# Six window-attention and gated-MLP layers behind a linear-attention layer: norm spreading and mask by 32-row tiles, one score product instead of two for a chunk's first 32 queries, no one-column products, K normalised behind the output projection

## Chip, core and metric

One core of one Trainium2 chip runs the whole program. The metric is the device time of one execution in microseconds (us). A core has five engines with queues of their own: PE (TensorE, matrix products), DVE (VectorE), ACT (ScalarE), POOL (GpSimd) and SP (SyncE, which issues all the DMAs here). They meet only through semaphores.

## What is computed

A token sequence of 2048 x 128 passes a linear-attention layer once and then six layers (DEPTH = 6) of local attention and a gated MLP. The changed part is in the local attention, 16 heads of 64, windows of 32 tokens that look one window back:

```python
q = l2norm(q) * qs
k = l2norm(k) * ksc
q = q * cos * scale + rotate_half(q) * sin * scale
inv = 1.0 / scale
k = k * cos * inv + rotate_half(k) * sin * inv
...
mask = (it < jb) | (it > jb + w) | (jb == -1)
sim = jnp.einsum('bhwie,bhwje->bhwij', bq, bk2) * QK_SCALE
sim = jnp.where(mask, -jnp.finfo(sim.dtype).max, sim)
attn = jax.nn.softmax(sim, -1)
out = jnp.einsum('bhwij,bhwje->bhwie', attn, bv2)
...
x = attn_layer(shift_tokens(x), Wqkv[i], q_scale[i], k_scale[i], Wo[i]) + x
x = ffn_layer(x, ...) + x
```

## The kernel before

The start (matrix names `m_...`) normalises the input and computes the linear attention of all 2048 tokens. Then a software pipeline runs over N = 48 blocks of T = 256 tokens (eight in each layer). One step of the pipeline is one block's projections (parts `a_...`), the attention of the block before it (`b_...`) and the MLP of the one before that (`c_...`). The order within a step is one table, SCHEDULE (line 57); every engine's code walks the same table and takes the parts that it has. EARLY (line 65) lists the parts of block 0 that are written out by hand in the start instead. All queues are in order.

The parts that matter here, for a block m:

- `a_v`, `a_x`, `a_y` (lines 414 to 459): V projection, and the two rotary halves of four head groups p = 0 to 3 (0 and 1 are K, 2 and 3 are Q), each into PSUM bank 0 (x) and bank 1 (y). Each operand is split in a high and a low part, so a product is three passes (`xh,wh`, `xh,wl`, `xl,wh`).
- `a_mx`, `a_my` (DVE, line 774) multiply the banks by the rotary tables into UV, `a_sqx`, `a_sqy` (ACT) square them, `a_rot` (POOL, line 1170) adds the halves into Kt or Qt.
- `a_norm` (line 461) sums the squares by head, `a_rck`, `a_lnk` make the inverse root R, `a_rh`, `a_rl` split it. `a_sp` (line 475) spreads R over the partitions with a selection matrix `sel`: part b fills bank b with four products of 128 rows. `a_kn` (DVE, line 818) multiplies Kt by bank b. Since banks 0 and 1 are taken by this, `a_x(m, 3)` waits for `a_kn(m, 0)` (semaphore khat_done) and `a_y(m, 3)` for `a_kn(m, 1)`.
- SP then copies the normalised K (`keys`, line 308: 8 DMAs, waits for both `a_kn`) and Q (`queries`, line 320: 8 DMAs) into the layout Kb, Qb, and V into the window layout V2 (`windows`, line 283: 16 DMAs, waits for `a_vs`).
- `b_s` (line 495): mask and scores of a chunk of 128 queries. The mask is added first, by products with an identity (`identb`), in 32x32 tiles, 8 for a chunk. The scores are 64 products a chunk and half (`i`) of 32 queries by 64 keys in 64x32 tiles. A chunk's first 32 queries of a block need the last 32 keys of the block before, kept apart in Kh, so they take two products of 32 keys each.
- `b_pt`, `b_pto` transpose the attention weights, `b_att` multiplies by V (64x64 tiles), `b_oto` (ACT) copies the result out, and `b_wo`, `c_wo` are the output projection. `b_att` begins chunks with a one-column product (line 550) that carries a wait.

On PE the order around the change is: `b_att`, `c_h0`, `a_sp0`, `a_sp1`, `b_wo`, `a_x3`, `a_y3`, `b_pt2`.

Of the kernel before, what the change touches and what calls it, by code (L numbers as in the profile page):

```python
# [17 lines left out]
P = 128  # L18
S = 2048
# [37 lines left out]
SCHEDULE = """a_vs0 a_v0 a_vs1 b_lnq a_sqy0 a_sqx0 b_rcq a_v1 a_mx0 a_rot0 a_x0 a_my0 b_sub0 b_rq w_h1 b_scale0 a_sqy1  # L57
    b_max0 c_xs b_exp0 a_mx1 a_rot1 a_y0 c_xb b_nrm0 c_zsq a_sqx1 a_halo a_xs+1 a_my1 c_rs b_sum0 b_s0 b_scale1
    a_lnk b_rqt b_s1 a_sqy2 a_x1 b_pto0 b_sub1 c_zh a_rh a_y1 c_wo c_zl b_s2 c_mu b_s3 c_var a_norm0 a_x2 b_pto1
    a_rl a_rck a_y2 b_pt0 b_exp1 a_rot2 a_sqx2 b_max1 b_oto0 c_zn a_mx2 a_my2 b_sum1 c_gelu0 b_pt1 b_att0 b_nrm1  # L60
    b_att1 c_h0 w_l0 a_sp0 a_rot3 a_kn0 w_h0 a_xh+1 a_sp1 b_wo a_kn1 a_xl+1 a_x3 a_sqy3 b_pto2 a_y3 b_pt2 c_hm0
    c_h1 a_mx3 a_my3 w_l1 b_att2 c_hm1 c_gelu1 b_xb a_sqx3 b_pt3 c_h2 b_pto3 c_hm2 a_norm1 c_gelu2 b_att3 c_wh
    c_wl w_h2 c_fin c_down w_l2 b_oto1""".split()
LAG = {"w": 0, "a": 0, "b": 1, "c": 2}
EARLY = """a_xs0 a_xh0 a_xl0 a_halo0 a_v0 a_vs0 a_v1 a_vs1 a_x0 a_y0 a_mx0 a_my0 a_sqy0 a_sqx0 a_rot0
    a_x1 a_y1 a_mx1 a_my1 a_sqy1 a_sqx1 a_rot1 a_norm0 a_sum0 a_rck0 a_lnk0 a_rh0 a_rl0 a_sp0 a_sp1 a_kn0 a_kn1""".split()
# [64 lines left out]
def program(nc, a):  # L131

    with ExitStack() as ctx:
# [19 lines left out]
        Kt = sb("Kt", [P, 2, HQ, T])  # L153
        Kb = sb("Kb", [P, HP, T])
        Kh = sb("Kh", [P, HP, W])
# [26 lines left out]
        identb = sb("identb", [P, P], BF16)  # L182
        ident = sb("ident", [P, P])
# [37 lines left out]
        Kst = Kt[:, :, :, :].rearrange("p h q t -> p (h q) t")  # L221
# [15 lines left out]
        def _(e):  # L237
# [98 lines left out]
            tables(1)  # L336
            keys(0)
            e.wait_ge(s["x1_done"], G1)
            e.dma_start(a["scratch"].rearrange("(c p) n -> p c n", p=P), xt).then_inc(s["scratch_out"], 16)
            e.wait_ge(s["scratch_out"], 16)  # L340
            for m in range(N):
# [7 lines left out]
                windows(m)  # L349
                if m:  # L350
                    keys(m)
# [16 lines left out]
        def _(e):  # L368
# [106 lines left out]
            def a_sp(m, b):  # L475

                e.wait_ge(s["rl_done"], m + 1)
                if b == 0:
                    e.wait_ge(s["sq_done"], m * 8 + (6 if m else 4))
                else:  # L480
                    e.wait_ge(s["mul_done"], m * 16 + (12 if m else 8))
                for i in range(2):
                    out = ps[:, b, i * T:(i + 1) * T]
                    mm(out, sel[:, 2 * b + i, :], Rh[:, :], True, False)
                    ins = mm(out, sel[:, 2 * b + i, :], Rl[:, :], False, True)
                ins.then_inc(s["rkb_done"], 1)
# [8 lines left out]
            def b_s(n, i):  # L495
# [5 lines left out]
                if i % 2 == 0:  # L501
# [28 lines left out]
            def b_pt(n, i):  # L530
# [597 lines left out]
        def _(e):  # L1128
# [126 lines left out]
```

## Time and profile before

| | |
|---|---|
| median of 3 runs | 1840.32 us (1836.89 to 1849.28) |
| the profiled execution's own time | 1832.69 us |
| span of the profile (first to last instruction) | 1831.1 us |
| busy: PE, DVE, ACT, POOL | 1654.4, 1217.9, 1139.4, 1000.9 us |
| mean granted TensorE clock | 0.969 of 2.4 GHz |

The profile is that of one execution. Busy time of PE is the union of its products' times; a product's end is modelled and overlaps the next ones, so for PE the distance from start to start is what to read. A product in fp32 stands as two instructions in the trace, so counts there are twice those of the code. "Idle before" is the engine's idle time ahead of an instruction, with what ended it. SPq rows are DMA issues of SP.

### The profile page before, as it was taken

What the parts mean: (1) busy time and instruction counts of PE and PEld (TensorE: products, weight loads), DVE (VectorE), ACT (ScalarE), POOL (GpSimd) and SP (SyncE); (2) the same over time, 40 slices, a digit from 0 to 9 for tenths busy, and PEclk for the clock granted to TensorE, in tenths of its full rate; (3) what the DMA queues carried; (4) which work ended last, traced back from release to release, by engine and by line L of the source; (5) the groups of instructions that cost most, each with busy time, mean ns of one, the idle gap of its engine ahead of it and who ended that gap; (6) DMA issues with size and microseconds to landing.
All of it is one profiled execution on the core that took longest, in us unless ns stands there. A gap on an engine that the chain in (4) does not pass through costs nothing.

```text
span 1831.1 us, 80253 instructions
## 1 busy us (share of the span) xinstructions
PE 1654.4 (90%) x35762; PEld 1360.0 (74%) x35762; DVE 1217.9 (67%) x1910; ACT 1139.4 (62%) x2115; POOL 1000.9 (55%) x757
## 2 busy tenths in 40 slices
PE   5858999989989998899999999999999989999986
PEld 4447778777777877778777787777778777778775
DVE  7656677666657766666766775676677676677562
ACT  2225676657656766666766666576566676667653
POOL 2135466656545656655674664585566475566441
PEclk9979999999999999999999999999999999999996
DMA  3085665665655567556557655557655665665650
GB/s 124 12 199 126 165 145 132 149 170 127 152 136 134 127 157 194 114 130 158 133 125 194 154 129 138 139 130 188 162 129 128 152 141 123 154 152 127 140 120 24
DMA packets 98585, 253.25 MB, mean 138 GB/s; under 512 B 30016, under 2 KB 36288, under 8 KB 97472
## 3 DMA queue, kind: packets, MB, share of 16 engines
q1 hardware_dynamic: 98240, 248.12, 56.8%
q8 instruction: 281, 4.60, 1.1%
q14 instruction: 64, 0.52, 0.1%
HBM read 44.59 MB, written 2.10 MB: 25 GB/s over the span
## 4 chain that ended last, share of the span: by engine, by line
PE 54%; DVE 11%; issue 9%; ACT 9%; SPq 8%; DMA 2%; POOL 0%; ACTq 0%; DVEq 0%; POOLq 0%
PE ps L370 49%; DVE E L841 4%; SPq L317 4%; PE ps L539 4%; SPq L328 4%; DVE rs L851 3%; DVE UV L780 2%; ACT E L930 2%; ACT zs L930 2%; DMA Qtb<-Qtb 2%; ACT PT L930 1%; ACT sq L930 1%; ACT Vs L930 1%; PE ps L492 1%; ACT R L930 1%
## 5 line engine op out<-in xcount | busy, mean ns | idle before, releaser
L780 DVE SCALAR_TENSOR_TENSOR UV<-ps,veca,rope 128x512 f32<-128x512 f32 x768 | 526.7, 743 | 192.4 <-PE ps L370 191.5
L1183 POOL TENSOR_TENSOR Kt<-UV 128x512 f32<-128x512 f32 x192 | 240.8, 1275 | 446.5 <-DVE UV L780 445.3
L930 ACT ACTIVATE sq<-ps 128x512 f32<-128x512 f32 (+1 forms) x400 | 231.5, 579 | 321.7 <-PE ps L370 303.4
L1183 POOL TENSOR_TENSOR Qtb<-UV 128x512 f32<-128x512 f32 x192 | 242.6, 1286 | 123.5 <-DVE UV L780 123.5
L1193 POOL TENSOR_TENSOR E<-E,mx 128x1024 f32<-128x1024 f32 x96 | 182.7, 1903 | 148.4 <-DVE mx L847 148.4
L370 PE MATMUL ps<-xh,wh 128*128 128x256 f32 x768 | 242.2, 315 | 6.0 <-issue 4.4
L370 PE MATMUL ps<-xh,wl 128*128 128x256 f32 x768 | 221.9, 289 | 1.8 <-issue 1.8
L370 PE MATMUL ps<-xl,wh 128*128 128x256 f32 x768 | 221.5, 288 | 1.9 <-issue 1.9
L370 PEld LDWEIGHTS ps<-PT,V 64*64 64x64 f32 x12288 | 198.7, 135 | 31.6 <-issue 19.3
L370 PE MATMUL ps<-Kb,Qtb 64*32 64x64 f32 (+1 forms) x12288 | 189.3, 223 | 34.6 <-issue 34.5
L370 PE MATMUL ps<-PT,V 64*64 64x32 f32 x12288 | 215.9, 221 | 1.5 <-ACT PT L930 0.7
L370 PEld LDWEIGHTS ps<-Kb,Qtb 64*32 64x32 f32 x12288 | 154.0, 106 | 63.2 <-issue 63.0
L370 PE MATMUL ps<-OT,wo 128*128 128x128 f32 x1536 | 194.8, 281 | 4.4 <-issue 4.4
L1202 POOL TENSOR_TENSOR E<-E,ri 128x1024 f32<-128x1024 f32 x96 | 182.8, 1905 | 21.8 <-DVE ri L853 21.6
L370 PEld LDWEIGHTS ps<-OT,wo 128*128 128x128 f32 x1536 | 187.5, 199 | 5.1 <-issue 4.9
L370 PEld LDWEIGHTS ps<-xh,wh 128*128 128x128 f32 x768 | 150.9, 196 | 49.6 <-issue 26.5
L930 ACT ACTIVATE Vs<-ps 128x512 f32<-128x512 f32 x192 | 114.6, 598 | 92.1 <-PE ps L370 73.3
L851 DVE TENSOR_REDUCE rs<-E 128x16 f32<-128x1024 f32 x96 | 117.1, 1220 | 62.3 <-ACT E L930 62.3
L841 DVE TENSOR_TENSOR E<-ps,rq 128x1024 f32<-128x1024 f32 x96 | 114.9, 1197 | 64.6 <-PE ps L370 64.2
L539 PE MATMUL ps<-ident,E 128*128 128x128 f32 x768 | 123.0, 283 | 37.5 <-ACT PT L930 35.2
L370 PEld LDWEIGHTS ps<-xl,wh 128*128 128x128 f32 x768 | 151.7, 198 | 4.0 <-issue 4.0
L370 PEld LDWEIGHTS ps<-xh,wl 128*128 128x128 f32 x768 | 151.9, 198 | 2.8 <-issue 2.7
(129 smaller groups left out, 3324.1 us busy)
## 6 DMA issues: line engine op xcount, KB each, us to landing
V<-Vs SPq DMA_DIRECT2D x672, 128.0 KB
Kb<-Kt SPq DMA_DIRECT2D x384, 128.0 KB
Qtb<-Qtb SPq DMA_DIRECT2D x384, 128.0 KB, 2.4
rope<-in_c_rope SPq DMA_DIRECT2D x48, 512.0 KB
raw<-in_Wqkv SPq DMA_DIRECT2D x6, 1536.0 KB, 6.9
V<-Vs SPq DMA_DIRECT2D x96, 64.0 KB
V<-V SPq DMA_DIRECT2D x96, 64.0 KB, 2.0
wo<-in_Wo SPq DMA_DIRECT2D x6, 512.0 KB, 5.9
```

Of the source, the lines that this page charges most:

```text
L317: e.dma_start(Kb[p0:p0 + W, j0:j0 + HQ, :], Kt[hq * W:(hq + 1) * W, half, :, :]).then_inc(s["k_in"], 16)
L328: e.dma_start(Qb[p0:p0 + W, j0:j0 + HQ, :], Qt[hq * W:(hq + 1) * W, half, :, :]).then_inc(s["q_in"], 16)
L370: return e.matmul(out, lhsT, rhs, start=start, stop=stop, **kw)
L492: ins = e.transpose(ps[:, NORM, T + c * P:T + (c + 1) * P], R[:, 1, c * P:(c + 1) * P], ident[:, :])
L539: ins = e.transpose(ps[:, PTB, h * P:(h + 1) * P], E[:, c, i % 2 * HQ + h, :, :], ident[:, :])
L780: e.scalar_tensor_tensor(UV[:, p % 2, slot, :].rearrange("p (i t) -> p i t", i=2), ps[:, half, :].rearrange("p (i t) -> p i t", i=2), veca ...
L841: e.tensor_tensor(E[:, c].rearrange("p j r k -> p r j k"), ps[:, 2:4, :].rearrange("p r (j k) -> p r j k", k=KEYS), by_row.unsqueeze(3).br ...
L851: e.tensor_reduce(rs[:, c], heads(E[:, c]), AX.X, ALU.add).then_inc(s["rs_done"], 1)
L930: return e.activation(out, in_, f, **kw)
L1183: e.tensor_tensor(dst, u, v, op).then_inc(s["rot_done"], 1)
L1193: e.tensor_tensor(ev, ev, mx[:, c].unsqueeze(2).broadcast_to([P, H, KEYS]), ALU.subtract).then_inc(s["sub_done"], 1)
L1202: e.tensor_tensor(ev, ev, ri[:, c].unsqueeze(2).broadcast_to([P, H, KEYS]), ALU.mult).then_inc(s["pn_done"], 1)
```

## The change

- `a_sp` is cut otherwise: part i now fills the i-th half of both banks, and a product reads only the 32 rows of R that it needs (a 32x128 tile at row 32q), high parts first and then low parts. Part 1 waits until part 0 is done. In the table it moves behind `b_wo`, and both `a_kn` behind it; each `a_kn` now waits for both parts.
- The mask of every chunk but the first of a layer is two products of 32 rows by 128 columns (with `fourb`, four identities side by side) instead of eight in 32x32 tiles.
- Kh, Kb and Kt become pieces of one tile KK, so that the last 32 keys of the block before and the first 32 of this one are read by one strided access: one score product instead of two for a chunk's first 32 queries.
- The one-column products go; their waits are on the second transposition of `b_pt`.
- At the start: in V2, block 0's V windows and the linear attention's output lie in different places; `windows(0)` is issued ahead of `keys(0)`; the wait for the copy to scratch stands at block 1; `a_x2`, `a_y2` and what belongs to them move ahead of `m_out(3)`; `m_sums(0)` ahead of `m_conv(0)`.

```diff
-    b_att1 c_h0 w_l0 a_sp0 a_rot3 a_kn0 w_h0 a_xh+1 a_sp1 b_wo a_kn1 a_xl+1 a_x3 a_sqy3 b_pto2 a_y3 b_pt2 c_hm0
...
+    a_sp0 a_rot3 w_h0 a_xh+1 b_wo a_sp1 a_kn0 a_kn1 a_xl+1 a_x3 a_sqy3 b_pto2 a_y3 b_pt2 c_hm0 c_h1 a_mx3 a_my3 w_l1
...
+    a_x1 a_y1 a_mx1 a_my1 a_sqy1 a_sqx1 a_rot1 a_norm0 a_sum0 a_rck0 a_lnk0 a_rh0 a_rl0 a_sp0 a_sp1 a_kn0 a_kn1
+    a_x2 a_y2 a_mx2 a_my2 a_sqy2 a_sqx2 a_rot2""".split()
...
-        Kt = sb("Kt", [P, 2, HQ, T])
-        Kb = sb("Kb", [P, HP, T])
-        Kh = sb("Kh", [P, HP, W])
+        KK = sb("KK", [P, HP * W + 2 * HP * T])
+        Kh = KK[:, 0:HP * W].rearrange("p (h k) -> p h k", h=HP)
+        Kb = KK[:, HP * W:HP * (W + T)].rearrange("p (h t) -> p h t", h=HP)
+        Kt = KK[:, HP * (W + T):HP * (W + 2 * T)].rearrange("p (x q t) -> p x q t", x=2, q=HQ)
+
+        def last_and_first(rows, h):
+            step = HP * W + h * (T - W)
+            return KK[rows, h * W:h * W + 2 * step].rearrange("p (a k) -> p a k", a=2)[:, :, 0:W]
...
-        xt = V2flat[:, 0:S].rearrange("p (c n) -> p c n", c=NCH)
-        xn = V2flat[:, S:2 * S].rearrange("p (c n) -> p c n", c=NCH)
-        wc = V2flat[:, 2 * S:2 * S + KLEPE * D].rearrange("p (i n) -> p i n", i=KLEPE)
-        lrow = V2flat[:, 2 * S + KLEPE * D:2 * S + 2 * KLEPE * D].rearrange("p (i n) -> p i n", i=KLEPE)
+        xt = V2flat[:, 3 * S:4 * S].rearrange("p (c n) -> p c n", c=NCH)
+        xn = V2flat[:, 0:S].rearrange("p (c n) -> p c n", c=NCH)
+        w0 = 2 * S + 512
+        wc = V2flat[:, w0:w0 + KLEPE * D].rearrange("p (i n) -> p i n", i=KLEPE)
+        lrow = V2flat[:, w0 + KLEPE * D:w0 + 2 * KLEPE * D].rearrange("p (i n) -> p i n", i=KLEPE)
...
+            windows(0)
             keys(0)
             e.wait_ge(s["x1_done"], G1)
             e.dma_start(a["scratch"].rearrange("(c p) n -> p c n", p=P), xt).then_inc(s["scratch_out"], 16)
-            e.wait_ge(s["scratch_out"], 16)
...
-                windows(m)
+                if m == 1:
+                    e.wait_ge(s["scratch_out"], 16)
                 if m:
+                    windows(m)
                     keys(m)
...
-            def a_sp(m, b):
-
-                e.wait_ge(s["rl_done"], m + 1)
-                if b == 0:
-                    e.wait_ge(s["sq_done"], m * 8 + (6 if m else 4))
+            def a_sp(m, i):
+
+                if i:
+                    e.wait_ge(s["rkb_done"], m * 2 + 1)
                 else:
-                    e.wait_ge(s["mul_done"], m * 16 + (12 if m else 8))
-                for i in range(2):
-                    out = ps[:, b, i * T:(i + 1) * T]
-                    mm(out, sel[:, 2 * b + i, :], Rh[:, :], True, False)
-                    ins = mm(out, sel[:, 2 * b + i, :], Rl[:, :], False, True)
+                    e.wait_ge(s["rl_done"], m + 1)
+                for x in range(2):
+                    for b in range(2):
+                        if x == 0 and i == 0 and b == 0:
+                            e.wait_ge(s["sq_done"], m * 8 + (6 if m else 4))
+                        elif x == 0 and i == 0:
+                            e.wait_ge(s["mul_done"], m * 16 + (12 if m else 8))
+                        q = 2 * b + i
+                        rows = slice(q * W, (q + 1) * W)
+                        ins = mm(ps[:, b, i * T:(i + 1) * T], sel[rows, q, :], (Rh, Rl)[x][rows, :], x == 0, x == 1,
+                                 tile_position=(q * W, 0))
                 ins.then_inc(s["rkb_done"], 1)
...
+                        if chosen:
+                            rows = slice(r * DH, r * DH + W)
+                            mm(ps[:, 2 + r, :].rearrange("p (j k) -> p j k", j=HP), fourb[rows, :],
+                               mask[rows, 1:2, :].broadcast_to([W, HP, KEYS]), True, False, skip_group_check=True,
+                               tile_position=(r * DH, 0))
+                            continue
                         for w in range(NW):
                             g = (w + r) % NW
-                            rows, v = slice(g * W, (g + 1) * W), chosen if chosen else 2 * r
+                            rows = slice(g * W, (g + 1) * W)
                             mm(ps[w * W:(w + 1) * W, 2 + r, :].rearrange("p (j k) -> p j k", j=HP), identb[rows, rows],
-                               mask[rows, v:v + 1, :].broadcast_to([W, HP, KEYS]), True, False, skip_group_check=True,
+                               mask[rows, 2 * r:2 * r + 1, :].broadcast_to([W, HP, KEYS]), True, False, skip_group_check=True,
                                tile_position=(g * W, w * W))
...
-                            spans = [(Kb[rows, h, c0 - W:c0 + W], 0, KEYS)] if c0 else [
-                                (Kh[rows, h, :], 0, W), (Kb[rows, h, 0:W], W, KEYS)]
-                            for k, k0, k1 in spans:
-                                ins = mm(ps[w * W:(w + 1) * W, 2 + r, h * KEYS + k0:h * KEYS + k1], Qb[rows, h, c0:c0 + W],
-                                         k, False, True, skip_group_check=True, tile_position=(r * DH, w * W))
+                            k = Kb[rows, h, c0 - W:c0 + W].rearrange("p (a k) -> p a k", a=2) if c0 else last_and_first(rows, h)
+                            ins = mm(ps[w * W:(w + 1) * W, 2 + r, h * KEYS:(h + 1) * KEYS].rearrange("p (a k) -> p a k", a=2),
+                                     Qb[rows, h, c0:c0 + W], k, False, True, skip_group_check=True,
+                                     tile_position=(r * DH, w * W))
...
+                    if i == 0 and h == 1:
+                        e.wait_ge(s["e_done"], n * C + C)
                     if i == 1 and h == HQ - 1:
                         e.wait_ge(s["v2_in"], n * 256 + 256)
+                    if i == 2 and h == 1:
+                        e.wait_ge(s["ots_done"], n * 4 + 2)
                     ins = e.transpose(ps[:, PTB, h * P:(h + 1) * P], E[:, c, i % 2 * HQ + h, :, :], ident[:, :])
                 ins.then_inc(s["pt_done"], 1)
 
             def b_att(n, i):
 
                 c, heads = i // 2, range(i % 2 * HQ, i % 2 * HQ + HQ)
-                if i == 0:
-                    e.wait_ge(s["e_done"], n * C + C)
-                elif i == 2:
-                    e.wait_ge(s["ots_done"], n * 4 + 2)
-                if i % 2 == 0:
-                    mm(ps[:, 2, 0:1], identb[:, :], identb[:, 0:1])
                 e.wait_ge(s["pts_done"], n * 4 + i + 1)
...
             a_v(0, 0)
+            m_sums(0)
             m_conv(0)
-            m_sums(0)
...
             a_sp(0, 0)
             a_sp(0, 1)
             m_gate(3)
+            a_x(0, 2)
+            a_y(0, 2)
             m_out(3)
...
+                e.tensor_copy(fourb[rows, :].rearrange("p (g k) -> p g k", g=NW),
+                              ident[rows, rows].unsqueeze(1).broadcast_to([W, NW, W])).then_inc(s["sel_done"], 1)
...
-                e.wait_ge(s["rkb_done"], m * 2 + b + 1)
+                e.wait_ge(s["rkb_done"], m * 2 + 2)
...
+            a_mx(0, 2)
+            a_my(0, 2)
...
+            a_sqy(0, 2)
+            a_sqx(0, 2)
...
+            a_rot(0, 2)
```

PE in one step of the pipeline, from the MLP's first product (`zh,w1`) to the Q projection `a_x3` (`xh,w`): before, the eight products of `a_sp` (`Rh,sel`, `Rl,sel`) stand together ahead of the output projection (`OT,wo`).

```order
L370 MATMUL ps<-zl,w1h 128x256
L370 MATMUL ps<-Rh,sel 128x256 [waits sq_done,rl_done]
L370 MATMUL ps<-Rl,sel 128x256
L370 MATMUL ps<-Rh,sel 128x256
L370 MATMUL ps<-Rl,sel 128x256
L370 MATMUL ps<-Rh,sel 128x256 [waits mul_done,rl_done]
L370 MATMUL ps<-Rl,sel 128x256
L370 MATMUL ps<-Rh,sel 128x256
L370 MATMUL ps<-Rl,sel 128x256
L370 MATMUL ps<-OT,wo 128x128 [waits ots_done,zn_done]
L370 MATMUL ps<-OT,wo 128x128 x7
L370 MATMUL ps<-xh,wh 128x256 [waits khat_done]
```

The same place of the changed kernel:

```order
L381 MATMUL ps<-zl,w1h 128x256
L381 MATMUL ps<-Rh,sel 128x256 [waits sq_done,rl_done]
L381 MATMUL ps<-Rh,sel 128x256 [waits mul_done]
L381 MATMUL ps<-Rl,sel 128x256 x2
L381 MATMUL ps<-OT,wo 128x128 [waits ots_done,zn_done]
L381 MATMUL ps<-OT,wo 128x128 x7
L381 MATMUL ps<-Rh,sel 128x256 [waits rkb_done]
L381 MATMUL ps<-Rh,sel 128x256
L381 MATMUL ps<-Rl,sel 128x256 x2
L381 MATMUL ps<-xh,wh 128x256 [waits khat_done]
```

Four of the eight products moved behind the output projection, and the next row is `a_x3` with its wait for khat_done, which DVE raises after `a_kn`.

SP's queue at the start, of before: the K copies (`Kb<-Kt`), the copy to scratch, and behind it the V windows (`V<-Vs`) and the Q copies.

```order
L281 DMA rope<-in_c_rope 128x1024 [waits u1_done,tab_in]
L317 DMA Kb<-Kt 32x1024 [waits k_halo,khat_done]
L317 DMA Kb<-Kt 32x1024 x7
L339 DMA scratch<-V 128x16x128 [waits x1_done]
L292 DMA V<-Vs 32x1024 [waits vs_done,scratch_out]
L292 DMA V<-Vs 32x1024 x3
L295 DMA V<-Vs 32x1024 x3
L297 DMA V<-Vs 32x512
```

The same queue of the changed kernel (the second half of the 16 V copies is left out):

```order
L290 DMA rope<-in_c_rope 128x1024 [waits u1_done,tab_in]
L301 DMA V<-Vs 32x1024 [waits vs_done]
L301 DMA V<-Vs 32x1024 x3
L304 DMA V<-Vs 32x1024 x3
L306 DMA V<-Vs 32x512
```

```order
L326 DMA KK<-KK 32x1024 [waits k_halo,khat_done]
L326 DMA KK<-KK 32x1024 x7
L349 DMA scratch<-V 128x16x128 [waits x1_done]
L337 DMA Qtb<-Qtb 32x1024 [waits rot_done]
L337 DMA Qtb<-Qtb 32x1024 x7
```

The V windows moved ahead of the K copies, and the Q copies now stand right behind the copy to scratch.

## Rows read from the trace of the kernel before

**Rows 1.** The page: busy time, share of the span and instructions by engine.
```profile
PE 1654.4 (90%) x35762; PEld 1360.0 (74%) x35762; DVE 1217.9 (67%) x1910; ACT 1139.4 (62%) x2115; POOL 1000.9 (55%) x757
```

**Rows 2.** Timeline of PE: start us, us, what, out<-in, count [idle before].
```profile
813.09 0.38 PE L370 MATMUL ps<-zh,w1h 128*128 128x256 f32 x1
...
813.90 0.28 PE L370 MATMUL ps<-Rh,sel 128*128 128x256 f32 x1
...
814.85 1.95 PE L370 MATMUL ps<-OT,wo 128*128 128x128 f32 x16
816.55 0.36 PE L370 MATMUL ps<-xh,wh 128*128 128x256 f32 x1
...
817.35 0.28 PE L370 MATMUL ps<-xh,wh 128*128 128x256 f32 x1
...
818.08 0.60 PE L539 MATMUL ps<-ident,E 128*128 128x128 f32 x4
...
819.22 0.18 PE L370 MATMUL ps<-identb 128*128 128x1 bf16 x1
819.41 1.14 PE L370 MATMUL ps<-PT,V 64*64 64x32 f32 x64
...
830.13 0.41 PE L370 MATMUL ps<-mask,identb 32*32 32x512 bf16 x8
830.47 0.21 PE L370 MATMUL ps<-Kh,Qtb 64*32 64x32 f32 x1
```

**Rows 3.** Timeline of DVE in the same step: `a_kn`.
```profile
814.58 2.35 DVE L824 TENSOR_TENSOR Kt<-ps,Kt 128x1024 f32<-128x1024 f32 x2
```

**Rows 4.** Timeline of ACT in the same step: `b_oto`.
```profile
813.29 1.08 ACT L930 ACTIVATE OT<-ps 128x512 f32<-128x512 f32 x2
```

**Rows 5.** Timeline of SP's queue in the same step: K and Q copies.
```profile
816.96 5.54 SPq L317 DMA_DIRECT2D Kb<-Kt  x8
822.60 5.77 SPq L328 DMA_DIRECT2D Qtb<-Qtb  x8
```

**Rows 6.** Who waited for whom: us in total, times, longest.
```profile
SPq L317 <- DVE Kt L824: 377.6, 48, 42.9
```
```profile
PE ps L370 <- issue: 52.8, 38, 3.3
PE ps L370 <- DMA Qtb<-Qtb: 14.4, 13, 4.7
```

**Rows 7.** Timeline of PE, score blocks and a change of tile shape.
```profile
831.43 0.44 PE L492 MATMUL ps<-ident,R 128*128 128x128 f32 x2
831.81 0.25 PE L370 MATMUL ps<-Kb,Qtb 64*32 64x64 f32 x3
...
838.49 0.86 PE L370 MATMUL ps<-Kb,Qtb 64*32 64x64 f32 x64
839.28 0.70 PE L370 MATMUL ps<-hid,mean 128*128 128x256 f32 x2
```

**Rows 8.** Timelines of SP, PE and POOL at the start of the pipeline.
```profile
97.98 0.58 SPq L339 DMA_DIRECT2D scratch<-V  x1
103.39 3.63 SPq L292 DMA_DIRECT2D V<-Vs  x4
...
114.68 5.04 SPq L328 DMA_DIRECT2D Qtb<-Qtb  x8
```
```profile
106.32 0.80 PE L370 MATMUL ps<-wh,xh 128*128 128x512 f32 x1 [2.39 <-POOL xl L1161]
...
116.73 0.80 PE L370 MATMUL ps<-wh,xh 128*128 128x512 f32 x1 [7.48 <-ACT Vs L930]
...
122.08 0.41 PE L370 MATMUL ps<-mask,identb 32*32 32x512 bf16 x8
```
```profile
103.09 2.49 POOL L1183 TENSOR_TENSOR Qtb<-UV 128x512 f32<-128x512 f32 x2 [0.54 <-DVE UV L780]
```

**Rows 9.** By stretch: us, busy (instructions) of PE, PEld, DVE, ACT, POOL; PEclk, DMA.
```profile
804.00:808.00 4.00, 3.92 (x31) 1.93 (x32) 2.12 (x4) 1.58 (x4) 1.90 (x1) 0.57 0.66 151
```

More of the change, by code:

```diff
@@ L54 @@
 PTB, WO, NORM, FF = 4, 5, 6, 7
[L57 to L60, printed above, removed]
-    b_att1 c_h0 w_l0 a_sp0 a_rot3 a_kn0 w_h0 a_xh+1 a_sp1 b_wo a_kn1 a_xl+1 a_x3 a_sqy3 b_pto2 a_y3 b_pt2 c_hm0
-    c_h1 a_mx3 a_my3 w_l1 b_att2 c_hm1 c_gelu1 b_xb a_sqx3 b_pt3 c_h2 b_pto3 c_hm2 a_norm1 c_gelu2 b_att3 c_wh
-    c_wl w_h2 c_fin c_down w_l2 b_oto1""".split()
+SCHEDULE = """a_vs0 a_v0 a_vs1 b_lnq a_sqy0 a_sqx0 b_rcq a_v1 a_mx0 a_rot0 a_x0 a_my0 b_sub0 b_rq w_h1 b_scale0 a_sqy1 b_max0
+    c_xs b_exp0 a_mx1 a_rot1 a_y0 c_xb b_nrm0 c_zsq a_sqx1 a_halo a_xs+1 a_my1 c_rs b_sum0 b_s0 b_scale1 a_lnk b_rqt
+    b_s1 a_sqy2 a_x1 b_pto0 b_sub1 c_zh a_rh a_y1 c_wo c_zl b_s2 c_mu b_s3 c_var a_norm0 a_x2 b_pto1 a_rl a_rck a_y2
+    b_pt0 b_exp1 a_rot2 a_sqx2 b_max1 b_oto0 c_zn a_mx2 a_my2 b_sum1 c_gelu0 b_pt1 b_att0 b_nrm1 b_att1 c_h0 w_l0
+    a_sp0 a_rot3 w_h0 a_xh+1 b_wo a_sp1 a_kn0 a_kn1 a_xl+1 a_x3 a_sqy3 b_pto2 a_y3 b_pt2 c_hm0 c_h1 a_mx3 a_my3 w_l1
+    b_att2 c_hm1 c_gelu1 b_xb a_sqx3 b_pt3 c_h2 b_pto3 c_hm2 a_norm1 c_gelu2 b_att3 c_wh c_wl w_h2 c_fin c_down w_l2
+    b_oto1""".split()
 LAG = {"w": 0, "a": 0, "b": 1, "c": 2}
 EARLY = """a_xs0 a_xh0 a_xl0 a_halo0 a_v0 a_vs0 a_v1 a_vs1 a_x0 a_y0 a_mx0 a_my0 a_sqy0 a_sqx0 a_rot0
-    a_x1 a_y1 a_mx1 a_my1 a_sqy1 a_sqx1 a_rot1 a_norm0 a_sum0 a_rck0 a_lnk0 a_rh0 a_rl0 a_sp0 a_sp1 a_kn0 a_kn1""".split()
+    a_x1 a_y1 a_mx1 a_my1 a_sqy1 a_sqx1 a_rot1 a_norm0 a_sum0 a_rck0 a_lnk0 a_rh0 a_rl0 a_sp0 a_sp1 a_kn0 a_kn1
+    a_x2 a_y2 a_mx2 a_my2 a_sqy2 a_sqx2 a_rot2""".split()
 def part(token):
@@ L182, in program @@
         identb = sb("identb", [P, P], BF16)
+        fourb = sb("fourb", [P, P], BF16)
         ident = sb("ident", [P, P])
@@ L220, in program @@
         sqf = sq[:, :, :, :].rearrange("p a b n -> p (a b) n")
-        Kst = Kt[:, :, :, :].rearrange("p h q t -> p (h q) t")
+        Kst = KK[:, HP * (W + T):HP * (W + 2 * T)].rearrange("p (x t) -> p x t", x=HP)
         SEMS = """const_in x_in b1_in scratch_out out_done
@@ L686, in _ @@
             m_conv(3)
-            e.wait_ge(s["sel_done"], 4)
+            e.wait_ge(s["sel_done"], 6)
             a_sp(0, 0)
@@ L721, in _ @@
             e.tensor_copy(identb[:, :], ident[:, :]).then_inc(s["sel_done"], 1)
+            for r in range(2):
+                rows = slice(r * DH, r * DH + W)
+                e.tensor_copy(fourb[rows, :].rearrange("p (g k) -> p g k", g=NW),
+                              ident[rows, rows].unsqueeze(1).broadcast_to([W, NW, W])).then_inc(s["sel_done"], 1)
             e.tensor_scalar(cen[:, :], ident[:, :], -1.0 / D, None, ALU.add).then_inc(s["sel_done"], 1)
@@ L1172, in a_rot @@
                 if p == 0:
-                    e.wait_ge(s["sel_done"], 4)
+                    e.wait_ge(s["sel_done"], 6)
                 if m == 0 and p == 2:
-                    e.wait_ge(s["x1_done"], G1)
+                    e.wait_ge(s["nm_done"], G1)
                 if m and p % 2 == 0:
```

## The prediction, as it was recorded

> **What bounds the kernel now.** First the page's busy shares: PE is busy in 90% of the span, no other engine above 67% [rows 1]. So I read PE's timeline next, start to start, in a step without a disturbance [rows 2]. From the MLP's first product at 813.09 to the second chunk's transposition at 818.08 PE starts one product after another and waits for nothing: 0.81 us of MLP, 0.95 for the eight products of `a_sp` (0.12 each), 1.70 for the output projection, 0.80 for `a_x3`, 0.73 for `a_y3`; together 4.99 us. Whatever holds PE up here is paid in full. The DVE timeline shows what these products hide: `a_kn` starts at 814.58 and its two instructions take 2.35 us, 1.18 each [rows 3]. They end at 815.76 and 816.93, before `a_x3` (816.55) and `a_y3` (817.35) need banks 0 and 1: a slack of 0.8 and 0.4 us.
>
> Then SP's queue. It waits for `a_kn`, 377.6 us in 48 waits [rows 6]: the K copies start at 816.96, just as the second `a_kn` ends, and take 5.54 us to issue; the Q copies stand behind them and take 5.77, to 828.37 [rows 5]. The first score product starts at 830.47, 2.1 us later, right behind the mask (830.13 to 830.47) [rows 2]. So a second loop is as long as PE's own: end of `a_kn`, then 13.5 us of copies, then scores. PE waits for Q only in 13 steps, 14.4 us in all [rows 6]: the two loops nearly tie.
>
> **The change, part by part.** Times are counted from the MLP's first product of the step.
>
> *K behind the output projection.* Before: `a_sp` 0.81, output projection 1.76, `a_x3` 3.46, `a_y3` 4.26, end 4.99. In the changed kernel the order of PE is four products of `a_sp`, output projection, the other four, `a_x3`, and each `a_kn` waits for all eight. The first four start at 0.81. Two of them read different rows and write different banks, so I let them lie beside each other: two rounds of 0.12, done by about 1.05 (not beside each other: 0.48, done by 1.29). The output projection can't follow before ACT has copied the attention's result, 813.29 + 1.08 = 814.37 [rows 4], which is 1.28; I take 1.32. So only 0.44 us of the shortening arrives. It ends at 3.02. The tile shape changes; the two transpositions of R between score blocks take 831.81 - 831.43 = 0.38 us where two products of that size take 2 x 1.70/16 = 0.21 [rows 2, 7], so two changes of shape cost 0.17, one 0.08. The last two products of `a_sp` start at 3.22 and take 0.28 [rows 2]: 3.50. `a_kn` runs from 3.54 to 4.72 and 5.89. `a_x3` starts at 4.77 instead of 3.46. `a_y3` starts at 5.94 instead of 4.26 (`a_x3` would let it go at 5.57), and ends at 6.67 instead of 4.99. The cover of `a_kn`, 1.70 us of output projection, is gone, and PE stands idle about 1.3 and then 0.4 us in every step. Cost: 1.68 us; if the tiles don't overlap, 1.97. The second `a_kn` ends at 5.89 instead of 3.84: 2.05 later. Behind the waiting `a_x3` PE's whole remaining step is queued, and behind `a_kn` on DVE the MLP's multiply, which is not needed for another 0.7 us.
>
> The page "TensorEngine Tiling (Array Packing)" of the Trainium skill says in its section Key Properties that a change of tiling mode drains the engine. This speaks against the change, which adds four changes of shape a step, and the trace agrees with 0.17 us for two. By that rule alone the new shape loses 0.34 a step, against a gain of at most 0.48; two of the four lie under the wait for ACT and for `a_kn`, and are not in the sum.
>
> *Scores.* A half of the first chunk takes 831.43 - 830.47 = 0.96 us with the split products, one of the second chunk 839.28 - 838.49 = 0.79 without [rows 2, 7]. Two halves: 0.34 us less a step. A strided read is in no row; the bounds are 0 and 0.34, and I take 0.34, since it reads as many keys.
>
> *Mask.* Eight products take 0.34 us [rows 2]. Two products of 512 columns: if 256 columns are 0.12 us, 0.24 beside each other and 0.48 one behind the other. I take 0; the bounds for two chunks are 0.2 less and 0.28 more.
>
> *One-column products.* One of two holds the next product up by 0.19 us [rows 2]. The change of shape that it also carries stays, so I take 0.1 each, 0.2 a step; bounds 0 and 0.38. The waits that move to `b_pt` are on work that is over by then (`b_oto` ended at 814.37, the transposition is at 818.08), so they cost nothing; if that cover went, PE would wait some tenths.
>
> *The step.* PE's own loop: 1.68 - 0.34 - 0.2 = 1.14 us longer (0.76 to 1.91 with the bounds). The loop over the copies: `a_kn` 2.05 later, scores 0.34 and one one-column product 0.1 shorter: 1.6 longer. It then is the longer loop by some 0.5 us, as far as it tied before. Between 1.14 and 1.6 I take 1.45, as the tie was near. Block 0's `a_kn` is in the start, so 47 steps: +68 us.
>
> *The start.* SP issues the copy to scratch at 97.98, and only at 103.39 the V windows, whose issue keeps the Q copies back to 114.68 [rows 8]. PE idles 7.48 us until ACT's V copy, which waits for the windows, and comes to the first mask at 122.08. In the changed kernel the windows go ahead of K. PE's work from the V projection (106.32) to the mask is then 15.76 - 7.48 = 8.3 us; the V projection waits for a POOL instruction behind the rotation that ends at 105.58 [rows 8], and the rotation comes about 2 us sooner with `a_x2` moved up. So the mask stands at about 112.6, and Q has landed by 103.6 + 5.04 + 2.1 = 110.7: 9.5 us sooner, a little more if the clock is up. I take -10, bounds -6 and -12.
>
> *The clock.* Its granted level was 0.57 between 804 and 808 [rows 9]: a stretch at 1.2 GHz that costs 4 x 0.43 = 1.7 us of PE's work, and it came after waits of PE. The new idle time will bring a few more; I take three, +5 us. Bounds: none, and one in each step.
>
> *Sum* against the profiled execution: 1832.69 + 68 - 10 + 5 = 1895.7 us, and 3 less for instruction waits (6% of 52.8, below). The median of the runs shown stands 7.6 us above that execution: **1900 us** for a median.
>
> **The rivals.**
>
> 1. *Not slower: instruction waits go away.* PE waits 52.8 us in 38 places for nothing that the profile shows ("issue") [rows 6]. I read them as instructions arriving late, most likely in the scores, where many short ones use them up fastest. The change removes in a step 32 split products, 12 mask products and 2 of one column, as the trace counts them: 46 of 35762/48 = 745 [rows 1], or 6%, most of it in the scores, and the new stop ahead of `a_x3` gives the supply time. If all 52.8 us went, 63 - 53 = 10 us would be left: no change, about 1850. With the low end of 0.76 us a step as well, 36 - 12 - 53 = -29: 1811, faster. It decides from some 45 us of these waits on. Against it: 6% is little, and the scores come some 12 us behind the stop.
> 2. *The clock falls in most steps.* At one fall in two steps 24 x 1.7 = 40 us more: 1940; at one a step 1975. For it: idle of 1.7 us within about 3 us in each step. Against it: the mean granted clock is 0.969 now, so falls are few although PE waits in places before the change too.
> 3. *The tiles don't overlap* (the change doesn't do what it says): 0.29 us x 47 = 14 us more, 1914. No row shows products on different rows of the same columns with 128 columns of weights. The page "TensorE: Matmul & The Clock Gate" of the Trainium skill, Part 3, lets a weight load overlap running products only when the row group differs, which it does here; by it the forecast stands and this rival falls. No row here shows it for this shape.
> 4. *The loop over the copies doesn't bind*: 1.14 us a step, 1886.
>
> **How the numbers follow.** The forecast has 0.40, rival 3 0.22, rival 4 0.10, rival 2 0.08, and rival 1 0.20, half of it within 1% and half faster. About 1% is what a measurement of this kernel can tell from no change. So slower by over 1%: 0.80, within 1%: 0.10, faster: 0.10. The range leaves out the faster half of rival 1, part of its other half, and the worst of rival 2: 1850 to 1938 us.
>
> **What would show it.** In the changed profile PE should idle about 1.3 us ahead of the first `xh,wh` product behind `Rl,sel` and 0.4 ahead of `a_y3`, both ended by DVE's `a_kn`, some 80 us in all; DVE should wait for PE ahead of `a_kn`; the section from the MLP's first product to the transposition should last 6.5 to 7 us; scores of the first chunk 0.79 us a half; waits for Q more than 14.4 us; the first mask near 112 us. If PE doesn't wait for `a_kn`, or the "issue" waits have shrunk to a few us, the forecast is wrong. If the step is right but the total is not, the start or the clock is.

## Result and profile after

| | before | changed |
|---|---|---|
| median | 1838.61 us (4 runs, 1834.79 to 1849.28) | 1890.45 us (4 runs, 1884.87 to 1900.04) |
| ratio, 95% interval | | 1.0281 [1.0238, 1.0324] |
| span of the profile | 1831.1 us | 1885.3 us |
| mean granted clock | 0.969 | 0.967 |
| first mask of the pipeline (start) | 122.1 us | 109.8 us |
| undisturbed step | 846.55 - 813.09 = 33.46 us | 966.30 - 931.00 = 35.30 us |

The change is slower, by 2.8%. It was forecast at 1900 us in a range of 1850 to 1938. The profiles differ by 54.2 us.

The timeline of PE in an undisturbed step of the changed kernel, to be laid beside [rows 2]: start us, us, what, out<-in, count, idle before.

```profile
931.00 0.39 PE L381 MATMUL ps<-zh,w1h 128*128 128x256 f32 x1
...
931.92 0.39 PE L381 MATMUL ps<-Rh,sel 32*128 32x256 f32 x2
932.14 0.28 PE L381 MATMUL ps<-Rl,sel 32*128 32x256 f32 x2
932.43 2.02 PE L381 MATMUL ps<-OT,wo 128*128 128x128 f32 x16
934.38 0.38 PE L381 MATMUL ps<-Rh,sel 32*128 32x256 f32 x2
934.61 0.28 PE L381 MATMUL ps<-Rl,sel 32*128 32x256 f32 x2
936.20 0.39 PE L381 MATMUL ps<-xh,wh 128*128 128x256 f32 x1 [1.32 <-DVE KK L849]
...
937.34 0.39 PE L381 MATMUL ps<-xh,wh 128*128 128x256 f32 x1 [0.15 <-DVE KK L849]
...
938.15 0.60 PE L564 MATMUL ps<-ident,E 128*128 128x128 f32 x4
...
966.30 0.39 PE L381 MATMUL ps<-zh,w1h 128*128 128x256 f32 x1
```

DVE in the same step answers [rows 3]:

```profile
934.92 2.36 DVE L849 TENSOR_TENSOR KK<-ps,KK 128x1024 f32<-128x1024 f32 x2 [2.56 <-PE ps L381]
937.20 0.47 DVE L909 SCALAR_TENSOR_TENSOR hid<-ps,vecc,hid 128x256 f32<-128x256 f32 x1
```

The stop, PE's idle time ahead of `a_x3`, stands where the prediction put it. The last `Rl,sel` pair starts at 934.61 and takes 0.28; `a_kn` starts at 934.92, having waited 2.56 us for PE, and PE stands idle 1.32 us ahead of `a_x3` and 0.15 ahead of `a_y3`. The idle figure ahead of `a_y3` is small because a product's modelled end runs into the gap; from start to start `a_x3` took 1.14 us instead of 0.80. The section from the MLP's first product to the transposition lasts 938.15 - 931.00 = 7.15 us, before 4.99.

The mask and the first chunk's scores in the same step, to be laid beside [rows 2] and [rows 7]:

```profile
950.27 0.39 PE L381 MATMUL ps<-mask,fourb 32*128 32x512 bf16 x2
950.59 0.86 PE L381 MATMUL ps<-KK,Qtb 64*32 64x64 f32 x64
951.38 0.44 PE L508 MATMUL ps<-ident,R 128*128 128x128 f32 x2
```

The mask takes 950.59 - 950.27 = 0.32 us and a half of the scores 951.38 - 950.59 = 0.79. SP's queue in this step, to be laid beside [rows 5]:

```profile
937.31 5.54 SPq L326 DMA_DIRECT2D KK<-KK  x8
942.94 5.68 SPq L337 DMA_DIRECT2D Qtb<-Qtb  x8
```

Who waited for whom, changed kernel, to be laid beside [rows 6]:

```profile
PE ps L381 <- DVE KK L849: 69.8, 95, 1.3
PE ps L381 <- issue: 21.6, 20, 3.1
PE ps L381 <- DMA Qtb<-Qtb: 11.2, 11, 3.5
```

The first line is the new wait: 69.8 us in 95 waits, none before. The second was not forecast in this size: "issue" waits fell from 52.8 to 21.6 us. The third says that the copies don't bind: 11.2 us, before 14.4. Most of the "issue" waits stand at the score products. These are the groups of PE in the kernel before (busy us, mean ns, idle before and what ended it):

```profile
L370 PE MATMUL ps<-Kb,Qtb 64*32 64x64 f32 x10752 | 189.1, 227 | 29.8 <-issue 29.7
L370 PE MATMUL ps<-Kh,Qtb 64*32 64x32 f32 x1536 | 90.2, 202 | 16.4 <-DMA Qtb<-Qtb 14.4 <-issue 2.1
L370 PE MATMUL ps<-Kb,Qtb 64*32 64x32 f32 x1536 | 88.1, 194 | 4.8 <-issue 4.8
```

and in the changed one:

```profile
L381 PE MATMUL ps<-KK,Qtb 64*32 64x64 f32 x12288 | 169.4, 225 | 24.4 <-issue 12.8 <-DMA Qtb<-Qtb 11.2
```

36.6 us before, 12.8 after.

The clock. By stretch of the changed kernel (us, busy time and instructions of PE, PEld, DVE, ACT, POOL, granted clock, DMA share, GB/s):

```profile
571.00:575.00 4.00, 2.52 (x20) 2.00 (x19) 3.14 (x4) 0.31 (x2) 1.03 (x1) 1.00 0.00 0
575.00:578.00 3.00, 3.00 (x40) 2.78 (x39) 2.40 (x5) 1.77 (x4) 1.25 (x2) 0.52 0.81 176
```

In the first stretch PE is busy 2.52 of 4 us, since the stop lies in it (there `a_x3` starts at 573.14); in the second the granted clock, 0.52, is at its lower level of 1.2 GHz nearly throughout. The same transposition and MLP products take

```profile
575.09 1.02 PE L564 MATMUL ps<-ident,E 128*128 128x128 f32 x4
575.76 0.56 PE L381 MATMUL ps<-zh,w1h 128*128 128x256 f32 x1
...
577.32 1.67 PE L381 MATMUL ps<-PT,V 64*64 64x32 f32 x64
```

0.67 and 1.56 us from start to start, where a step at the full level has 0.36 and 0.98. I count the stretches at the lower level in the trace's clock records that begin between 122 us and the last V projection: 10 with 44 us before, 23 with 82 us in the changed kernel. All numbers of low clock below are counted so. Start and end of the program had more of it before, which is why the mean clock hardly moved (0.969 and 0.967).

### The profile page after: what moved, and what is told of

Its sections match the earlier page's. It is cut to its first block and busy times, and to the rows that moved or that the text cites. A ratio compares the mean times of both kernels' runs of the same rounds, so it can differ in the third digit from the quotient of the medians.

```text
span 1885.3 us, 75862 instructions
## 1 busy us (share of the span) xinstructions
PE 1677.8 (89%) x33590; PEld 1339.8 (71%) x33590; DVE 1220.2 (65%) x1912; ACT 1142.1 (61%) x2115; POOL 1000.4 (53%) x757
## 5 line engine op out<-in xcount | busy, mean ns | idle before, releaser
L1212 POOL TENSOR_TENSOR KK<-UV 128x512 f32<-128x512 f32 x192 | 241.6, 1279 | 443.8 <-DVE UV L805 443.7
L381 PE MATMUL ps<-xh,wh 128*128 128x256 f32 x768 | 245.7, 320 | 71.1 <-DVE KK L849 69.8
L381 PEld LDWEIGHTS ps<-PT,V 64*64 64x64 f32 x12288 | 203.6, 138 | 41.0 <-issue 31.4
L381 PE MATMUL ps<-PT,V 64*64 64x32 f32 x12288 | 221.2, 223 | 1.5 <-ACT PT L957 0.7
L849 DVE TENSOR_TENSOR KK<-ps,KK 128x1024 f32<-128x1024 f32 x96 | 113.1, 1220 | 125.6 <-PE ps L381 125.6
L381 PEld LDWEIGHTS ps<-OT,wo 128*128 128x128 f32 x1536 | 182.6, 194 | 13.8 <-issue 13.5
L381 PE MATMUL ps<-KK,Qtb 64*32 64x64 f32 x12288 | 169.4, 225 | 24.4 <-issue 12.8
L381 PEld LDWEIGHTS ps<-KK,Qtb 64*32 64x32 f32 x12288 | 136.2, 105 | 72.9 <-issue 56.3
L564 PE MATMUL ps<-ident,E 128*128 128x128 f32 x768 | 133.7, 301 | 37.8 <-ACT PT L957 35.3
```

Source lines behind the costliest of these rows:

```text
L381: return e.matmul(out, lhsT, rhs, start=start, stop=stop, **kw)
L849: e.tensor_tensor(k, r.broadcast_to([P, 2, 2, T]), k, ALU.mult).then_inc(s["khat_done"], 1)
L1212: e.tensor_tensor(dst, u, v, op).then_inc(s["rot_done"], 1)
```

## The experiments

Times are medians; ratios are against the kernel before on the same chip, with a 95% interval. Its median there was 1843.82 us beside kernels 1 to 4, 1839.01 beside 5 to 8 and 1843.64 beside 9. Waits and sections are read in each run's profile.

### 1 and 2: the changed kernel with the order, and with the whole spreading, of before

```diff
-    a_sp0 a_rot3 w_h0 a_xh+1 b_wo a_sp1 a_kn0 a_kn1 a_xl+1
+    a_sp0 a_rot3 a_kn0 w_h0 a_xh+1 a_sp1 b_wo a_kn1 a_xl+1
```

> The changed kernel with one part undone: the table's order of before, so that all of a_sp stands ahead of the output projection and a_kn lies beside it. My theory (PE's own loop sets the step, and the place of a_sp and a_kn is the whole cost): the section from the MLP's first product to the transposition falls from 7.15 to about 5.3 us, no wait of PE for a_kn is left, and 47 steps give some 87 us, less what instruction waits (21.6 us in the changed kernel, 52.8 before) grow again: 1800 to 1825 us. Rival A (the loop over K and Q copies sets the step): the copies still start earlier by as much, so the time falls too, but PE then waits for Q in most steps, over 20 us in all. Rival B (the 32-row tiles and their changes of shape are the cost): the section stays above 6 us and the time above 1860.

Measured: 1778.96 us, ratio 0.964 [0.9607, 0.9673]. A step of it on PE:

```profile
881.11 0.39 PE L381 MATMUL ps<-zh,w1h 128*128 128x256 f32 x1
...
882.03 0.39 PE L381 MATMUL ps<-Rh,sel 32*128 32x256 f32 x2
...
882.60 0.39 PE L381 MATMUL ps<-Rh,sel 32*128 32x256 f32 x2
...
883.03 2.05 PE L381 MATMUL ps<-OT,wo 128*128 128x128 f32 x16
884.84 0.36 PE L381 MATMUL ps<-xh,wh 128*128 128x256 f32 x1
...
886.37 0.60 PE L564 MATMUL ps<-ident,E 128*128 128x128 f32 x4
```

The section is 5.26 us, no wait for `a_kn` is left, and the kernel is 111 us faster than the changed one. That is more than I gave it (65 to 90 us). The section accounts for 47 x (7.15 - 5.26) = 89 us; the low clock fell from 82 to 7 us as well, which at half the clock can be worth at most half of the 75 us. Rival A falls, though not by much: waits for Q are 18.4 us, in 20 waits, where it asked for over 20 us and most steps. Rival B falls too.

The second kernel also takes `a_sp` and the wait of `a_kn` from the kernel before:

```diff
-            def a_sp(m, i):
+            def a_sp(m, b):
...
-                e.wait_ge(s["rkb_done"], m * 2 + 2)
+                e.wait_ge(s["rkb_done"], m * 2 + b + 1)
```

> The changed kernel with the norm spreading of before in shape and place (eight products of 128 rows ahead of the output projection, each a_kn behind its own four); all else is new. If the 32-row tiles gain nothing because of the changes of shape (0.52 us for four tiles plus 0.25 at the output projection behind them, against 0.95 for eight), this is some 0.3 us a step faster than the same order with 32-row tiles: 1785 to 1810 us, section 5.0 us. If overlapping tiles are worth their price, it is equal or slower than that kernel, above 1810.

Measured: 1753.01 us, ratio 0.9502 [0.9473, 0.9531], below what I gave it. The same section lasts 844.27 - 839.28 = 4.99 us:

```profile
839.28 0.39 PE L381 MATMUL ps<-zh,w1h 128*128 128x256 f32 x1
...
841.05 1.94 PE L381 MATMUL ps<-OT,wo 128*128 128x128 f32 x16
842.75 0.36 PE L381 MATMUL ps<-xh,wh 128*128 128x256 f32 x1
...
844.27 0.60 PE L559 MATMUL ps<-ident,E 128*128 128x128 f32 x4
```

This version beats both kernels, by 4.98% and 7.3%. The spreading by 32-row tiles, as it is cut here, is a loss by itself: 26 us in the medians, 20 in the profiles. Of these 47 x 0.27 = 13 are the section, and 8 the waits for Q, 10.4 us here and 18.4 there. The two parts have different causes. The tiles do lie beside each other: the two products of a pair start 4 ns apart. But four pairs take 883.03 - 882.03 = 1.00 us, no less than the 0.95 of eight whole products: the first part takes 0.57, since the second waits for its end, and the second 0.43. And the products around them get longer: the MLP's ahead of them take 0.92 instead of 0.82, the output projection behind them 1.81 (884.84 - 883.03) instead of 1.70 (842.75 - 841.05). In the changed kernel, where such tiles stand on both sides of it, it takes 1.95 (934.38 - 932.43). The waits for Q belong to the cut: each pair fills a part of both banks, so both `a_kn` wait for all pairs. `a_kn` starts 2.03 us into the section there and 1.49 here, and the copies behind it move by the same 0.54 us.

### 3: the move alone, in the kernel before

```diff
-    a_sp0 a_rot3 a_kn0 w_h0 a_xh+1 a_sp1 b_wo a_kn1 a_xl+1
+    a_sp0 a_rot3 w_h0 a_xh+1 b_wo a_sp1 a_kn0 a_kn1 a_xl+1
...
-                e.wait_ge(s["rkb_done"], m * 2 + b + 1)
+                e.wait_ge(s["rkb_done"], m * 2 + 2)
```

> The kernel before with the move alone: the table's new order, each a_kn waiting for both parts; spreading, mask, scores, one-column products and start as before. My theory: the section grows from 4.99 to about 6.8 us, 87 us in 47 steps, and some 15 us of clock falls: 1925 to 1945 us. What it tells apart beside that is why the instruction waits fell from 52.8 to 21.6 us in the changed kernel: if the new stop of PE gives the supply time, they fall here too, to some 25 us, and the time is about 1910; if it is the 6% fewer instructions, they stay near 50 and the time is 1930 or more.

Measured: 1957.1 us, ratio 1.0623 [1.058, 1.0666], above what I gave it. Who waited for whom in this kernel:

```profile
PE ps L370 <- DVE Kt L824: 68.7, 91, 1.3
PE ps L370 <- issue: 54.6, 39, 4.7
```

The timeline of its section:

```profile
929.88 0.39 PE L370 MATMUL ps<-zh,w1h 128*128 128x256 f32 x1
...
935.13 0.39 PE L370 MATMUL ps<-xh,wh 128*128 128x256 f32 x1 [1.32 <-DVE Kt L824]
...
936.26 0.38 PE L370 MATMUL ps<-xh,wh 128*128 128x256 f32 x1 [0.15 <-DVE Kt L824]
...
937.08 0.60 PE L539 MATMUL ps<-ident,E 128*128 128x128 f32 x4
```

The section is 7.20 us, 2.21 longer, or 104 us in 47 steps; the low clock rose from 44 to 82 us, 38 us more, worth at most 19. The profile is 119.9 us longer. The "issue" waits stayed at 54.6, so the stop does not take them away.

### 4, 6 and 7: the product edits, in the kernel before

Kernel 4 has the one score product, the mask of 128 columns and no one-column products; kernel 6 only the first, kernel 7 only the second. The start, the spreading and the order are those of before; the edits are the hunks of the diff in `b_s`, `b_pt` and `b_att`. All three have K in the one tile KK and make `fourb` at the start.

```diff
                             rows = slice(r * DH, (r + 1) * DH)
-                            spans = [(Kb[rows, h, c0 - W:c0 + W], 0, KEYS)] if c0 else [
...
+                            k = Kb[rows, h, c0 - W:c0 + W].rearrange("p (a k) -> p a k", a=2) if c0 else last_and_first(rows, h)
```

> The kernel before with the product edits alone: one score product instead of two for a chunk's first 32 queries, mask by 32-row tiles of 128 columns, no one-column products; spreading, order and start as before. By the sections in the changed kernel 0.34 us a step for the scores, 0.04 for the mask and nothing for the one-column products: 18 us, 1820 us. If the fewer instructions are what lowers the instruction waits, these fall from 52.8 to some 25 us here and the time is 1785 to 1800; if the stop of PE does it, they stay near 50 and it is 1815 to 1825.

> The kernel before with the one score product instead of two alone (32 of the 46 instructions that the product edits remove from a step, all in the first chunk's scores). All three product edits together gave about 61 us in the profile: 18 in the products themselves, 30 in instruction waits (52.9 to 23.2 us), 14 in clock falls. Theory A (instructions are used up too fast in the first chunk's two score blocks, and those waits go with the 32 products there): 16 us in the products, most of the waits gone, 1775 to 1795 us. Theory B (the number of instructions in a step counts, wherever they are): waits fall by 32/46 of 30, about 20 us, 1795 to 1805 us. Theory C (where the stream's pieces of the instruction memory happen to fall): the waits stay, about 1822 us.

> The kernel before with the mask by 32-row tiles alone (12 of the 46 instructions of a step fewer). In the products themselves 0.04 us a step, 2 us. Theory A of the scores' run (the first chunk's score blocks): the waits stay near 50 us, 1835 us. Theory B (the number): 8 us less in waits, 1825 to 1830. Theory C (where the pieces fall): anything between 1790 and 1840, with no relation to the number removed.

| | time, us | ratio | "issue" waits of PE, us (times) | of these at score products | low clock in the pipeline, us |
|---|---|---|---|---|---|
| before | | | 52.8 (38) | 36.6 | 44 |
| 4, all three | 1771.36 | 0.9594 [0.9559, 0.9629] | 23.6 (23) | 11.4 | 14 |
| 6, scores | 1789.55 | 0.9721 [0.9692, 0.975] | 33.9 (35) | 14.7 | 17 |
| 7, mask | 1831.53 | 0.9961 [0.9929, 0.9993] | 51.6 (36) | 35.8 | 55 |

Who waited for whom in kernel 4, 6 and 7, in this order:

```profile
PE ps L377 <- issue: 23.6, 23, 3.0
PE ps L377 <- issue: 33.9, 35, 2.7
PE ps L377 <- issue: 51.6, 36, 4.1
```

The groups of PE in kernel 6, score products and the head sums of `a_norm`:

```profile
L377 PE MATMUL ps<-KK,Qtb 64*32 64x64 f32 x12288 | 170.8, 224 | 33.8 <-DMA Qtb<-Qtb 18.7 <-issue 14.7
L377 PE MATMUL ps<-sq,ind 128*32 128x256 f32 x1536 | 106.9, 390 | 7.2 <-issue 5.8 <-ACT sq L940 1.4
```

Edits that make the products 0.4 us a step shorter (18 us) took 61 us off the profile. Another 29 us of it are instruction waits, and 30 us less of the low clock can be worth at most 15. The two go together in part: the low stretch of [rows 9] in the kernel before comes right behind an "issue" wait of 1.08 us ahead of a score product at 804.08. The score edit alone takes 19 of the 29 us of waits, the mask edit 1; the rest, 9 us, goes only in the kernel that has all three edits. No kernel has the one-column products out by themselves, or the scores with one of the other two, so these 9 us can't be given to an edit.

By kernel 6 alone theory B had it as well: it put the fall of the waits at about 20 us, and 19 were measured. Against it speak kernel 7, where it wanted 8 us and got 1, and kernel 9 below. For theory A speaks the place: at the score products the waits fell from 36.6 to 14.7 us, 22 us, while 5.8 us of new ones came up at `a_norm`'s products, which the kernel with all three has at 1.3. So theory A is the nearest, but "most of the waits gone" was too much. Theory C has little for it: kernels 3, 5 and 7 shift the stream as well, and their waits are 54.6, 57.5 and 51.6 us. The one-column products, taken out, gain nothing: the transpositions and the MLP's products ahead of `b_att` got longer by just the 0.1 and 0.19 us that they had taken. That was the change of shape.

### 5: the start alone, in the kernel before

```diff
+            windows(0)
             keys(0)
```

> The kernel before with the start of the changed kernel alone (V windows issued ahead of K, scratch waited for at block 1, a_x2 and a_y2 moved up). The changed kernel's first mask stands at 109.8 us, that of before at 122.1. My theory: 12 us less and nothing else, 1825 to 1832 us, steps and waits of the pipeline as before.

Measured: 1825.79 us, ratio 0.9924 [0.9897, 0.995]: 14 us less. The first mask stands at 108.05 us instead of 122.08; the shortest step is unchanged. The forecast of 12 us lies inside the interval.

### 8 and 9: the changed kernel with its idle time filled

Products that nobody reads, behind the second part of `a_sp`, into the bank of the transpositions: five of 512 columns, or 46 of 32 columns in 32x32 tiles. Nothing of the computation is left out.

```diff
                 ins.then_inc(s["rkb_done"], 1)
+                if i and m:
+                    for x in range(5):
+                        mm(ps[:, PTB, :], sel[:, x % HQ, :], sel[:, :, :])
```

> The changed kernel with five products of 512 columns that nobody reads, put into the idle time ahead of a_x3 (into the PSUM bank of the transpositions, about 0.23 us each). The stop itself stays: a_x3 still waits for a_kn. My theory: the stop costs twice, once as idle time and once through the clock, which is at its lower level for 82 us of the pipeline against 41 before. With the idle time filled the falls mostly go, the shortest step stays at 35.2 us, and the time falls by 20 to 37 us, to 1855 to 1872 us. Rival (the falls come from elsewhere, or the filling delays a_x3): no change or some us more, 1885 to 1900 us.

Measured: 1871.78 us, ratio 1.019 [1.0143, 1.0236], against 1.0281 [1.0238, 1.0324] without the filling: the intervals just miss each other, and the slowest of its four runs (1886.30) lies above the changed kernel's fastest (1884.87). The stop itself is as in the changed kernel, and so is the shortest step (35.2 us). PE's timeline at the filling:

```profile
899.69 0.28 PE L381 MATMUL ps<-Rl,sel 32*128 32x256 f32 x2
899.90 1.43 PE L381 MATMUL ps<-sel 128*128 128x512 f32 x5
901.29 0.39 PE L381 MATMUL ps<-xh,wh 128*128 128x256 f32 x1
```

`a_x3` starts 1.82 us behind `a_sp`'s second part (901.29 - 899.47), as without the filling (936.20 - 934.38). Yet the low clock went from 82 to 14 us, in 3 stretches instead of 23, and the time by some 19 us (15 in the profiles). That is the second price of the stop: it is paid through the clock. (The expectation's 41 us for the kernel before are 44 by the count used here.) At half the clock 68 us can be worth at most 34. Part of what came back went into longer waits for Q (who waited for whom):

```profile
PE ps L381 <- issue: 23.9, 21, 3.4
PE ps L381 <- DMA Qtb<-Qtb: 22.6, 22, 3.7
```

22.6 us against 11.2; 15 + 11 + 2 ("issue") = 28 of the 34 us are so accounted for. The copies are the next bound, close behind.

> The changed kernel with 46 small products that nobody reads (32x32 tiles, 32 columns, bf16) in the idle time ahead of a_x3. They bring a step back to the number of instructions of before, 745 as the trace counts them, in a place where PE waits anyway. Theory B (the number in a step sets the instruction waits, wherever the instructions are): the waits rise from 21.6 us to 45 to 55, and the time by some 30 us, to 1910 to 1925 us. Theory A (only how densely the first chunk's score blocks use instructions up): the waits stay at 15 to 30 us; the time stays at 1880 to 1900 us, or falls a little where the small products keep the clock up as the large ones did.

Measured: 1874.66 us, ratio 1.0173 [1.0112, 1.0235]. Who waited for whom in this kernel:

```profile
PE ps L381 <- DVE KK L853: 49.3, 94, 0.9
PE ps L381 <- issue: 20.6, 22, 3.0
```

With the number of instructions of before the "issue" waits are 20.6 us, as without them. Theory B falls: the number in a step, wherever they are, is not what counts. What is left is where they stand. The low clock was 34 us in 10 stretches: the small products took 48 us of it away, the large ones 68. The time agrees with the other filled kernel's.

## Why the prediction was right

The sign, the size and the place came out as forecast, and the mechanism, the lost cover of `a_kn`, is shown. That 1890 came so near to 1900 is in part luck: the step was put 18 us too low and the clock some 6 us, and the fall of the instruction waits was put 28 us too small, and these misses cancel.

- *PE's own loop sets the step, and `a_kn` behind the projection stops it.* Right, and shown both ways: undone in the changed kernel it takes 113 us off the profile, alone in the kernel before it adds 120. The section was put at 6.67 us and is 7.15. Of the missing 0.48, 0.36 stand at the output projection: it takes 1.95 us, not 1.70, and it starts 1.43 us into the section, not 1.32. I had priced a change of shape at 0.08.
- *The loop over the copies binds, 1.6 us a step.* Wrong: waits for Q went down to 11.2 us. I had read the two loops as tied. In the step shown the Q copies' issue ended at 828.37 and the first score product started at 830.47, 2.10 us later, but over all steps the shortest such distance is 1.80; so there were 0.3 us to spare. In the changed kernel it is 1.97 (948.62 to 950.59). The copies themselves start 2.44 us later in the section (937.31 - 931.00 against 816.96 - 813.09), more than my 2.05. A step grew by 1.84 us because of the section alone: 2.16 longer, less 0.34 for the scores and 0.04 for the masks leaves 1.78. My 1.45 was taken between a PE loop that I had too short (1.14) and a copy loop that does not bind; that it came within 0.4 of the 1.84 is not the reasoning's merit. The upper bound of 1.91 that I gave for PE's loop was also added up with the scores' 0.34 in it; with their own bound of 0 it is 2.25. That the two loops are near each other was right, as the filled kernel shows.
- *Scores.* 0.79 us a half, as forecast. *Mask.* 0.32 us for 0.34, where I took no gain. *One-column products.* 0, not 0.2; the change of shape was the whole of it.
- *Tiles beside each other* (rival 3). They do lie beside each other; the rival falls, but so does the gain that I took for granted: the two pairs of `a_sp`'s second part take 883.03 - 882.60 = 0.43 us in kernel 1, where four whole products take 0.48 and I had let pairs take 0.24. The rule of the page "TensorE: Matmul & The Clock Gate", Part 3, of the Trainium skill, that weight loads overlap running products only where the row group differs, agrees with the trace: the two products of a pair, on different row groups, started 4 ns apart. The rule of the page "TensorEngine Tiling (Array Packing)", Key Properties, of the Trainium skill, that a change of tiling mode drains the engine, agrees with the longer rows beside the tiles (0.92 for 0.82, 1.81 and 1.95 for 1.70). The sum leaned on tile overlap and gave the changes of shape too little.
- *The start.* Forecast -10, measured -12.3 in the first mask's place, just past my bound of -12.
- *The clock.* Forecast +5 us by three more falls; the pipeline had 13 more, 38 us more at the lower level, worth at most 19. Filling the stop takes away 68 us of it and some 19 us off the whole. This is rival 2 in small: 13 more falls in 47 steps.
- *Instruction waits.* Forecast -3 us, measured -31. This is rival 1, at three fifths of its strength. I had counted the instructions removed and not asked where they stood: the score edit took out a fifth of the instructions in the two densest blocks (16 of 80 each). The size of this term was the largest miss, and it is what kept the result below my 1900. The stop, which I had named as a second reason for it, has no part in it (54.6 us in kernel 3).

The profiles' 54 us, then: 47 x 1.84 = 86 for the step, -12 for the start, -31 for instruction waits, which leaves 11 for the clock and the rest. I didn't measure this last part by itself; half of the 38 us more at the lower level, 19 us, bounds the clock's share from above.

What stays open: what makes the "issue" waits. That instructions arrive late is my reading; the runs show only that thinning out the scores takes them away. No run shows why the removal of the mask's and the one-column products takes 9 us more of them beside the scores' edit, when the mask's alone takes 1, and the one-column products were never removed alone.

## What to carry to other kernels

When an engine's queue is full, ask what covers a dependent operation before moving it: here 1.7 us of output projection, with the products right ahead of and behind it, covered 2.35 us of VectorE work, and moving the producer behind the cover cost 1.9 to 2.2 us a step, and some more through the clock. Count as a gain of smaller tiles only what is left when the products on both sides have paid for the change of shape. And judge a bundle of edits part by part: of this one the product edits and the start were worth 5%, and the moved spreading took more than that back.

## What the runs showed that I had not expected

- Removing 32 of 745 PE instructions a step from the densest stretch of small products took 19 of 52.8 us of "issue" waits; adding 46 in a stretch where the engine waits anyway added no waits (21.6 to 20.6 us).
- Products that nobody reads, put into a wait, made the kernel about 1% faster: 82 us at the lower clock became 14.
- The output projection (16 instructions of 128x128) takes 1.70 us among products of 128 rows, 1.81 with 32x128 tiles ahead of it, and 1.95 with such tiles on both sides.
- Two overlapping pairs of 32x128 tiles took 0.43 us at best, four whole products 0.48.
- A one-column product between different tile shapes costs nothing by itself: without it, its 0.1 and 0.19 us stand ahead of the next product.
